# A two-layer decoder on one core: the last layer's routing and dense experts written into the 128-wide attention's loop, and a new order in the causal attention

## What is computed

```python
# L1_attn: 16 heads of 16, causal
scores = jnp.where(causal, -1e9, scores); a = softmax(scores); ctx = a @ v
# L1_xattn: 16 query heads, 4 key heads of width 128, over context and own tokens,
# root mean square norm of q and k, rotary angles, then @ Wo.T
# L1_ffn: 64 experts of width 64, the best 8 of each token, and a shared expert
logits = x @ gate_w.T
topv, topi = jax.lax.top_k(logits, TOP_K)
W = zeros.at[n, topi].set(softmax(topv))
inter_w = silu(gate) * up * W[:, :, None]
out = einsum('nei,ehi->nh', inter_w, dp_w) + sigmoid(x @ sh_gate1_w.T) * shared
```

## Time and profile before

| | before |
|---|---|
| median of 3 runs | 962.25 us |
| profiled execution: its time | 963.12 us |
| its span, first to last instruction | 961.3 us |
| TensorE busy | 808.9 us (84%) |
| VectorE, ScalarE, POOL busy | 654.4, 542.8, 291.7 us |
| mean granted TensorE clock | 0.927 |
| causal attention (a1), with the wait at its start | 317.6 to 420.1 us |
| 128-wide attention | 421.1 to 657.5 us |
| routing of the last layer | 657.1 to 692.6 us |
| experts | 692.6 to 952.8 us |

### The profile page before, as it was taken

The page is one execution under the profiler, slowest core; times in us unless marked ns, Lnnn a source line. Parts: engine busy times, 40 slices in busy tenths (PEclk is TensorE's granted clock), DMA queues, the critical chain, the costliest instruction groups (busy, mean ns, idle before and its releaser), DMA issues. The chain is left out here.

```text
span 961.3 us, 16618 instructions
## 1 busy us (share of the span) xinstructions
PE 808.9 (84%) x5626; PEld 538.1 (56%) x5626; DVE 654.4 (68%) x1412; ACT 542.8 (56%) x1697; POOL 291.7 (30%) x254
## 2 busy tenths in 40 slices
PE   3898887549996088868999999996499999999996
PEld 2677765428875066634577777785244444444443
DVE  3774588849883279728999999864465656656554
ACT  1777765238775056526878778772445554455442
POOL 1111245730001555408644544500212222222220
PEclk9998998579999599959999999997599999999999
DMA  9960001228994112000000000001164444444421
GB/s 304 397 268 2 2 13 45 77 83 288 318 319 160 56 49 63 2 0 1 1 1 2 1 2 1 1 2 53 43 165 116 115 115 115 115 115 123 120 85 44
DMA packets 35408, 90.81 MB, mean 94 GB/s; under 512 B 6407, under 2 KB 8970, under 8 KB 34827
## 3 DMA queue, kind: packets, MB, share of 16 engines
q1 hardware_dynamic: 32266, 81.63, 26.4%
q0 software_dynamic: 3072, 8.30, 2.7%
HBM read 67.71 MB, written 22.29 MB: 94 GB/s over the span
## 5 line engine op out<-in xcount | busy, mean ns | idle before, releaser
L1312 POOL TENSOR_TENSOR m1ws<-m1raw,m1ws 128x768 f16<-128x768 f32 x33 | 55.0, 1670 | 218.6 <-ACT m1raw L1315 218.6
L1544 ACT ACTIVATE m1ap<-m1ac 128x512 f16<-128x512 f32 x66 | 41.6, 630 | 115.8 <-DVE m1ac L1628 115.8
L1622 DVE TENSOR_TENSOR m1sg<-m1sg,m1Wb 128x512 f32<-128x512 f32 x66 | 61.1, 926 | 63.7 <-ACT m1sg L1540 53.1
L1582 PE MATMUL m1pg<-m1hs,m1ws 128*128 128x512 f16 x396 | 97.5, 383 | 3.8 <-PEq L60 3.8
L1593 PE MATMUL m1py<-m1ap,m1ws 128*128 128x512 f16 x396 | 96.2, 379 | 1.9 <-DVE m1ap L1634 1.9
L1582 PE MATMUL m1pu<-m1hs,m1ws 128*128 128x512 f16 x396 | 96.3, 379 | 0.0
L922 POOL TENSOR_TENSOR xqr<-xqr,xt 128x512 f32<-128x512 f32 x48 | 67.6, 1416 | 67.5 <-DVE xt L1203 67.5
L1634 DVE TENSOR_TENSOR m1ap<-m1ac,m1ap 128x512 f16<-128x512 f32 x66 | 45.7, 692 | 45.9 <-ACT m1ap L1544 45.9
L1582 PEld LDWEIGHTS m1pg<-m1hs,m1ws 128*128 128x128 f16 x396 | 38.9, 98 | 51.4 <-issue 5.4
L1678 POOL DMA_INDIRECT rows<-slots_out,slot x32 | 32.7, 1023 | 114.0 <-DMA slots_out<-m0yo 101.4
L1593 PEld LDWEIGHTS m1py<-m1ap,m1ws 128*128 128x128 f16 x396 | 38.6, 98 | 49.2 <-DVE m1ap L1634 2.9
(11 more groups left out here) (291 smaller groups left out, 1964.3 us busy)
## 6 DMA issues: line engine op xcount, KB each, us to landing
m1Wb<-wt_dram SPq DMA_DIRECT2D x66, 256.0 KB, 3.9
m1raw<-in_m_w SPq DMA_DIRECT2D x33, 384.0 KB, 4.3
...
m0xg<-slots_in SPq DMA_DIRECT2D x32, 256.0 KB, 3.6
slots_out<-m0yo SPq DMA_DIRECT2D x32, 256.0 KB, 3.1
...
```

The costliest lines, as they stand in the source:

```text
L1312: pool.tensor_tensor(ws[:, u, 1, :], raw[:, u, :], ws[:, u, 0, :], ALU.subtract).then_inc(prep_ok, 1)
L1582: ins = pe.matmul(bank[:, :], part(ws, u, sw, c, which), hs[:, sh, c, CH * q:CH * q + CH], start=(k == 0), stop=(k == 5))
L1622: dve.tensor_tensor(sg[:, q, :], sg[:, q, :], Wb[:, u, CH * q:CH * q + CH], ALU.mult).then_inc(sw_ok, 1)
```

## The change

In the causal attention all four engines get a new list: steps are offset by up to three tiles, keys and queries are separate steps (`keys`, `queries`), `v_copy` goes from VectorE to ScalarE, so do the two small casts at the start, and the setting of V2 goes from POOL to VectorE behind the first tile's `norm_a`. `fetch` is issued in halves of two DMAs around `root`, and all eight rope products are in the loop, one for each tile.

`attention128` and `moe_dense` become one function, `attention_and_experts`, with one block and no barrier in between. Routing of a tile (`route_stats`, `route_root`, `route_norm`, `route_turn`, `route_rows`, `route_low`, `logits`, `logits_out`) is done tile by tile in the loop some three tiles behind; the lower half of the turned tile is now made on POOL (`route_low`) and no longer on VectorE. The choice of experts (`highest`, `others`, `shares`) is done for tiles 0 to 3 and for tiles 4 to 7 apart, each with its own turn, copy, DRAM write and loads of the broadcast rows. The first six `hidden` steps run first half of pairs 0, 1, 2, then second half of pairs 0, 1, 2, and the first two stand among the last tile's attention steps. PSUM and SBUF of the attention are reused under other names: below, `red` is the tile that holds the split activations, `rows` the raw weights and logits, `xqr`, `xt`, `xsq` what was m1sg, m1ac, m1ap. The steady loops over tiles have a new order on PE, ACT, DVE and POOL. The amount of arithmetic is as before.

```diff
             if slots:
-
-                pool.wait_ge(zeroed, 3)
+                slots.fetch(pool, 1, 0)
                 for n in range(NT):
+                    if n + 1 < NT:
+                        slots.fetch(pool, n + 1, 1)
                     root(n)
                     if n + 2 < NT:
-                        slots.fetch(pool, n + 2)
-                        if n < 4:
-                            slots.rope.product(pool, (2, 3, 6, 7)[n])
-                for i in (0, 1, 4, 5):
-                    slots.rope.product(pool, i)
...
+            if causal:
+                act.activation(ident16[:, :], ident[:, :], ACT.Copy)
+                act.activation(cmask16[:, :, :], bcast(C["cmask"][:, :], 1, HG), ACT.Copy).then_inc(ready, 1)
+                for n in range(-3, TILES):
+                    at(n, ct_copy)
+                    at(n + 3, h_out)
+                    at(n + 1, pt_copy)
+                    at(n + 2, exps)
+                    at(n + 3, q_copy)
+                    at(n + 2, v_copy)
+                return
...
+                for n in range(-3, TILES):
+                    at(n, pv)
+                    at(n + 2, queries)
+                    at(n + 1, values)
+                    at(n + 2, scores)
+                    at(n, turn_ctx)
+                    at(n + 3, turn)
+                    at(n + 1, turn_probs)
+                    at(n, project)
+                    at(n + 3, keys)
+                return
...
+            if causal:
+                for n in range(-2, TILES + 2):
+                    at(n, k_mask)
+                    at(n + 1, norm_b)
+                    at(n - 2, o_norm)
+                    if n + 2 < TILES:
+                        slots.add(dve, n + 2)
+                    at(n, soft)
+                    at(n - 2, residual)
+                    at(n + 2, norm_a)
+                    if n == -2:
+                        dve.memset(V2[:, :, :, :, :], 0.0).then_inc(zeroed, 1)
+                        dve.wait_ge(zeroed, 1)
+                        for par in range(2):
+                            col = par * (HD + 1) + HD
+                            dve.memset(V2[64 * par:64 * par + 64, :, :, :, col:col + 1], 1.0).then_inc(zeroed, 1)
+                return
             dve.wait_ge(zeroed, 3)
...
-def attention128(nc, C, w):
...
+def attention_and_experts(nc, C, w, w_a1, rows, a, out):
...
+            for q in range(NCH):
+                cols = slice(CH * q, CH * q + CH)
+                copied(sp, "W", q)
+                sp.dma_start(wt_dram[:, cols], WT[q]).then_inc(stored, 16)
+                sp.wait_ge(stored, 16 * q + 16)
+                for p in range(NR):
+                    load_b(p, p, cols, b_in[p] if q else b_first[p])
+                if q == 0:
+                    for p in range(NR):
+                        sp.wait_ge(prep_ok, p + 1)
+                        load_raw(p + NR, p)
+            for p in range(NR):
+                sp.wait_ge(sw_ok, NR + p + 1)
+                load_b(p + NR, p, slice(0, B * S), b_in[p])
+
...
+            def prep_high(p):
+                act.wait_ge(w_in[p % NR], 16 * (p // NR) + 16)
+                if p >= NR:
+                    act.wait_ge(y_ok, p + 1)
+                act.activation(ws[:, p % NR, 0, :], raw[:, p % NR, :], ACT.Copy, scale=W_UP)
+                act.activation(raw[:, p % NR, :], raw[:, p % NR, :], ACT.Copy, scale=W_UP).then_inc(high_ok1, 1)
+
...
+            def hidden(j, p, u, q, k):
+
+                pe.wait_ge(prep_ok, p + 1)
+                if type(j) is int and j == 0:
+                    pe.wait_ge(rope_ok, NT * 6)
+                    pe.wait_ge(v_out, NT * 2)
+                    pe.wait_ge(rlow_ok, HALF)
+                elif type(j) is int and j == 1:
+                    pe.wait_ge(exp_ok, NT * 4)
+                else:
+                    pe.wait_ge(act_ok, j - 1)
+                if type(j) is int and j == NR:
+                    pe.wait_ge(rlow_ok, NT)
...
+            project(7, 0)
+            project(7, 1)
+            project(7, 2)
+            project(7, 3)
+            route_turn(6)
+            logits(5)
+            hidden(2, *early(2))
+            route_turn(7)
+            logits(6)
+            logits(7)
+            down(0, *early(0))
+            hidden(3, *early(3))
+            turn_shares(1)
+            hidden(4, *early(4))
+            down(1, *early(1))
+            hidden(5, *early(5))
+            down(2, *early(2))
+            down(3, *early(3))
+            down(4, *early(4))
+            hidden(6, 3, 0, 0, 0)
+            down(5, *early(5))
+            def pair(p, u, r):
+                hidden(p * 2 + 1, p, u, 1, 1)
...
+            act_high(1, 1)
+            route_exps(1)
+            silu(2, 0)
+            shares_out(1)
+            act_high(2, 0)
+            silu(3, 1)
+            silu(4, 0)
+            act_high(3, 1)
+            prep_high(3)
+            silu(5, 1)
+            act_high(4, 0)
+            act_high(5, 1)
+            prep_high(4)
...
-    def fetch(self, pool, n):
+    def fetch(self, pool, n, *halves):
+
         if n >= NROWS:
             pool.wait_ge(self.summed, K0 * (n - NROWS + 1))
-        for k in range(K0):
+        for k in [2 * half + i for half in halves or (0, 1) for i in range(2)]:
             pool.indirect_dma_start(self.rows[:, n % NROWS, k, :], None, self.C["slots_out"],
```

More of the change, by code:

```diff
@@ new lines, in part, with early, over_pairs, is_pair @@
+        def part(u, s, c, which):
+            k = P * (2 * c + which)
+            return ws[:, u, s, k:k + P]
+        def early(j):
+            return j % NR, j % NR, j // NR, j % 2
+        def over_pairs(eng, body):
+            with eng.Fori(0, NPAIR // NR - 2) as i:
+                for u in range(NR):
+                    body(i * NR + (NR + u), u, i + 1)
+            for u in range(NR):
+                body(NPAIR - NR + u, u, NPAIR // NR - 1)
+        def is_pair(p):
+            return type(p) is not int or p < NPAIR
@@ L1093, in pv @@
                 u = n % 2
[L1094 removed]
+                copied(pe, f"P{k}", n)
                 if k == 1:
@@ new lines, in down @@
+            def down(j, p, u, q, k):
+                first, last = (type(p) is int and p == i for i in (0, NPAIR - 1))
+                if type(j) is int and j == 0:
+                    pe.wait_ge(x_ok, NT)
+                    pe.wait_ge(o_out, 4 * NT)
+                elif type(j) is int and j == NR:
+                    copied(pe, "W", 1)
+                    copied(pe, "L", NT - 1)
+                pe.wait_ge(al_ok, j + 1)
+                for c in range(DC):
+                    for i, (sw, sa) in enumerate(PASSES):
+                        ins = pe.matmul(p_y[c][q][:, :], ws[:, u, sw, GU + P * c:GU + P * c + P], ap[:, k, sa, :],
+                                        start=(first and i == 0), stop=(last and i == 2), skip_group_check=True)
+                ins.then_inc(y_ok, 1)
@@ new lines, in _ @@
+            route_stats(4)
+            maxes(6, 3)
+            scale(7, 4)
+            normalise(6, 1)
+            normalise(6, 2)
+            scale(7, 5)
+            highest(0)
+            residual(5)
+            o_low(6, 0)
+            normalise(6, 3)
+            maxes(7, 0)
+            o_low(6, 1)
+            route_norm(4)
+            maxes(7, 1)
+            others(0)
+            o_low(6, 2)
+            normalise(7, 0)
+            shares(0)
+            maxes(7, 2)
+            o_low(6, 3)
```

1007 lines of the change are left out of this document (569 added, 438 removed).

## The result

The changed kernel takes 937.04 us (median of 4 runs, 932.93 to 941.74), the one before 961.95 in the same session. The ratio is 0.9737, with a 95% interval of 0.9688 to 0.9787: faster, by 20 to 30 us. The forecast of 927 was 10 us too low, the range of 912 to 939 held it, and the forecast case's own range of 918 to 935 did not. The profiled execution took 932.93 us, span 931.2; it is the fastest of the four.

The account below looks back on a forecast made before the run. TensorE bounds the 128-wide attention and experts; gains lie where it stands, in routing and causal attention. 963.1 - 15 (causal) - 20 (handover) = 928.1, median 927, range 912 to 939.

Parts of the forecast that it names:

- Start of the causal attention: Causal attention's start: VectorE no longer waits for V2, and POOL's first root comes 4.9 us earlier.
- Its loop: Causal attention's steady loop: mean tile falls from 9.3 to 8.2 us, gain 7.7 us.
- the ring: Causal loop: queries copied behind exponentials, then scores, turn and probabilities' copy, tie ScalarE and TensorE at 7.8 us a tile.
- Its drain: Causal attention's end: extra queueing behind older tiles' steps could give up to 5 us or nothing; 2.4 taken.
- The 128-wide loop: 128-wide attention: 28.2 us a tile with TensorE full, about 1 us a tile of it added by the routing.
- that rival: 128-wide loop: VectorE becomes the bound, 1.5 us for each of six tiles, giving 936; chance 0.12.
- Stalls: TensorE waits behind the last projection: shares' turn 1.0, `hidden` 4 1.6, `hidden` 5 3.0, `down` 4 4.4; together 10 us.
- At clock 1.00: Behind the last projection: TensorE's four waits, about 10 us together, pass with the granted clock at 1.00.
- the 20 forecast for the handover: Attention to experts: 37.9 us available, less 7 routing work, 10 stalls and 1 tail, gives 20 us.
- the table's drain: Second half's routing chain: table switches cost more than their row, up to 1.5 us twice, giving 930; chance 0.10.
- A handover of 18 us: Behind the last projection: stalls of 18 us instead of 10, giving 935; chance 0.10.
- The ring of two banks: 128-wide loop: late normalised rows stop TensorE at turns sharing two PSUM banks; at 6 us a tile 975; chance 0.03.

Follow-up runs that it names:

- kernel 6: Kernel 3 with expert steps 3, 4 and 5 of the second half reading the first half's broadcast shares (output wrong): 927.76 us.
- kernel 3: The kernel after, with ScalarE scaling pair 3's weights behind `silu` 5 and `act_high` 4, and VectorE's lower half of 4 ahead of `times_up` 5: 930.54 us.
- kernel 7: Kernel 3 with the second half's two exponentials replaced by plain copies, so no table switch there (shares wrong): 933.91 us.

## Why the prediction was right, and where it was off

- **Start of the causal attention, 4.9 us:** right. The root comes 5.05 us earlier against the first fetch.
- **Its loop, 7.7:** too high. From first to last root 64.63 - 58.70 = 5.9. The mechanism was named, products beside slot sums on every tile, but 8.2 us for a tile was chosen too low: the mean is 8.39, since 1.43 to 2.52 us are added to six of eight sums, and one `norm_b` ahead of the last root loses 1.6. That mean is made of unlike tiles; three of seven take 9.2, though the loop as a whole does not stay above the 9 us that was named as a sign of being wrong. Without the products it is the ring at 7.76.
- **Its drain, 2.4:** from the last root to the last residual 27.43 - 24.65 = 2.8. Right. In sum 13.8 for 15. The upper bound given for the stage, 23, should have been 24.6 by its own terms (4.9 + 14.7 + 5); nothing hangs on it.
- **The 128-wide loop, 28.2 for a tile with TensorE full:** 27.67, since a turn of 0.22 and logits of 0.39 are 0.6 and not 1 us. VectorE is not the bound; that rival is out. But 3.9 us of waits come in the last tiles; the kernel before has 0.8 there, so 3.1 are new where 1 was allowed. Of the 13.7 by which X grew, the trace gives 5.2 to two `hidden` steps, 3.7 to the routing's matmuls ahead of t0 (six turns of 0.22, five logits of 0.39, one turn of shares of 0.43) and 3.1 to these waits; 1.7 is left and not taken apart. This is a mis-sized term: the forecast read each tile as the steady one and didn't follow the lists where the loop's order ends.
- **Stalls, 10:** 1.0, 1.6, 3.0 and 4.4 were 0.82, 1.38, 2.56 and 5.32, with 0.45 that wasn't seen. Right, each with its cause: 3 shown by kernel 6, 4 by kernel 3; 1 goes in kernel 7, and 2 is read from rows alone. Stall 4 is 0.9 longer than forecast, and `weigh` 5, 1.0 longer than usual beside GpSimd, accounts for that. The second half's shares are there at 671.01, 16.9 behind t0, where 17.5 was said. Of the two table loads' 2.6 us only 0.75 lay on the chain to the first of them (kernel 7).
- **At clock 1.00:** wrong. The prediction said that TensorE stands at four places "at clock 1.00"; the clock fell behind two of the waits, 3.8 us in the profiled run, a cost that the forecast put at nothing. That the wait of 5.32 brings it is shown by kernel 3, which loses both; the 1.5 us at `hidden` 5 came in this execution and not in the second profile of the same kernel. With 2.1 in the last tiles (3.1 for 1) and 0.5 in the stalls these make 6.4 of the 6.5 us between the 20 forecast for the handover and the 13.5 that E and X give. That they meet so closely is luck in part: the 1.7 us left over in X stand in none of them, so something else came out smaller by as much.
- **The rest:** 1.2 + 6.5 = 7.7 of the 10 us. The other 2 to 3 lie between execution and median: the profiled execution of the kernel after is the fastest of its four, 4.1 us under their median, that of before 1.2 over its own, and 2.8 of this is in the start already taken off.
- **The rivals:** the table's drain is refuted by rows. A handover of 18 us was not reached, but 10.5 of waits and 3.8 of clock lie half way to it. The ring of two banks never held a tile up.
